# A recommendation tower on one core: ScalarE takes over the normalization of 12 of 26 features

## The chip, the core and the metric

The kernel runs on one core of a Trainium2 chip. The core has five engines that run side by side and meet through semaphores: TensorE (PE; its weight loads are PEld), VectorE (DVE), ScalarE (ACT), GpSimd (POOL) and SyncE (SP). The metric is the device time of one launch in microseconds (us), lower is better. Three runs of the kernel before took 626.68, 628.12 and 629.10 us.

## What is computed

The batch has 2048 samples, each with a dense vector of 256 numbers and 26 table lookups of 64 numbers (all float32). Cut to what matters:

```python
e = stack([tbl_f[ids[:, f]] for f in range(26)], axis=1)          # 2048 x 26 x 64
x = layer_norm(dense @ Wd.T, gd, bd)                              # 2048 x 128
y = layer_norm(einsum('bnd,ed->bne', e, Ws), gs, bs)              # each feature projected and normalized
y = layer_norm(einsum('bne,pn->bep', y, Wsi), gsi, bsi)           # 26 features mixed into 32
T = concat([x, y])                                                # 33 vectors of 128
Z = T @ T^T, its lower triangle (528)                             # pairwise products
out = layer_norm(Zflat @ Wl.T, gl, bl), the first 384 of 512
h = relu([out, dense] @ W_top1 + b_top1); h = relu(h @ W_top2 + b_top2); y = h @ W_top3
```

The first layer norm of a feature needs a factor per sample and feature, one over a standard deviation. The kernel finds that deviation without projecting: it takes a quadratic form of the gathered row, and then scales the gathered row itself. That scaling, row times factor, is what the change moves.

## The kernel before

**Tiles and quarters.** The 2048 samples are 16 tiles `t` of 128 (one sample per partition). Every engine runs the same outer loop, `for h in range(QUARTERS)`, over quarters `h`, 83 in all. A tile enters at `h = 4t` and passes through stages at fixed distances (the constants `MEASURE = 1` to `STORE = 22`), so that some six tiles are in work at once. `tile(h, at)` gives the tile whose once-per-tile stage `at` falls into this quarter, `part(h, at)` the tile and the quarter (0 to 3) of a stage that comes four times per tile. There is no scheduler: each engine executes its steps in the order in which they are written in its loop, and waits where a semaphore has not come far enough. In this text "quarter 0 to 3" is `h` modulo 4; a tile's norms fall into `h = 4t+1` to `4t+4`.

**Gathers (L255).** GpSimd issues 26 indirect DMAs per tile, one per feature, into `emb[t % 2]`, in four batches of 8, 6, 6 and 6. A batch waits for `gram_done` (the pairwise products of some eight quarters back) and for `nrm_ready` (that the buffer's last user, two tiles back, has been read).

**Norms.** TensorE transposes the gathered batch into `b_a` (L312), ScalarE copies it to `embt` (L494), TensorE multiplies with a Gram matrix into `b_a` (L321), VectorE multiplies with `emb` (`prod`, L757) and sums (`var_n`, L761); every second quarter it clips the result (`var_m`, L767) and ScalarE takes the root (`std_n`, L500).

**Normalization.** VectorE's `normalize(t, k)` takes the reciprocals (`rstd_n`, L774) and scales two features per instruction into `nrm` (L778): seven instructions for features 0 to 13 (k = 0) in quarter 3, six for features 14 to 25 (k = 1) in the quarter 1 two quarters later. `nrm` is laid out as 64 x 32, features innermost, so each feature is written at steps of 32 numbers (128 bytes). Then `shuffle(t)` transposes `nrm` into `byn` (L788), which the mixing of the following four quarters reads.

**Mixing and projection, four times per tile.** TensorE mixes into `b_mix` (L330), ScalarE copies to `mixed` (L505), TensorE projects into `b_y` (L342), VectorE adds the bias (`yb`, L793), ScalarE squares (`sq`, L510), VectorE sums (`var_y`, L800), ScalarE takes the root (`std_y`, L515, a quarter later), VectorE takes the reciprocal (L805) and scales into `V` (L811, four instructions), TensorE forms the products `b_z` (L354), ScalarE copies to `zs` (L521).

**Once per tile.** The dense vector's branch ends in ScalarE's `xn` (L541, quarter 3), TensorE's transpose of it (L377), and ScalarE's `V` (L551) and `xt` (L554) at the head of quarter 0. In quarter 0 VectorE also rearranges `zs` (L822 to L825). TensorE interacts in quarter 1 (L396, ten matmuls), and runs the top network's layers (L418, L425, L434) for an older tile over all four quarters; this begins at `h = 18`. ScalarE's `zt` (L559, L561) and `h` (L586, L592) belong to them. In the first eleven quarters VectorE also prepares weights.

TensorE's order inside a quarter is: transpose of `xn`, transposes of the batch, mixing, norms, projection, layers, products. `b_a` and `b_mix` are single buffers, so ScalarE's copies stand between TensorE's steps.

Of the kernel before, what the change touches and what calls it, by code (L numbers as in the profile page):

```python
# [35 lines left out]
HALVES = [range(0, 14), range(14, 26)]  # L36

# [4 lines left out]
DENSE_NORM = 3  # L42
# [28 lines left out]
def tower(nc, a, out):  # L71
# [4 lines left out]
    with ExitStack() as ctx:  # L76
# [6 lines left out]
        def sem(name):  # L83
# [68 lines left out]
        prod_done, varn_done, varm_done, stdn_done, rstdn_done, nrm_ready, byn_ready = (  # L152
            sem("prod_done"), sem("varn_done"), sem("varm_done"), sem("stdn_done"), sem("rstdn_done"), sem("nrm_ready"), sem("byn_ready"))
# [88 lines left out]
        def _(pool):  # L242
# [4 lines left out]
            for t in range(T):  # L247
                if t < 2:
                    pool.wait_ge(idx_loaded[t], 16)
                for b in range(4):  # L250
                    after(pool, nrm_ready, 2 * (t - 2) + b // 2 + 1)

                    after(pool, gram_done, 4 * t + b - PROJECT - 2)
                    for f in features(b):
                        pool.indirect_dma_start(out=emb[t % 2][:, f, :], out_offset=None, in_=tables[f],  # L255
                                                in_offset=bass.IndirectOffsetOnAxis(ap=idx[:, t, f:f + 1], axis=0)
                                                ).then_inc(gathered[t % 2][b], 16)
# [220 lines left out]
        def _(act):  # L478
# [22 lines left out]

            def copy_mixed(t, c):
                act.wait_ge(mix_done, 4 * t + c + 1)
                after(act, proj_done, 4 * t + c - 1)
                nc.scalar.activation(mixed[c % 2][:, :], b_mix[:, :], ACT.Copy).then_inc(mixed_copied, 1)  # L505
# [92 lines left out]
            for h in range(QUARTERS):  # L598
# [13 lines left out]
                if (last := part(h, PROJECT + 2)):  # L612
                    copy_zs(*last)
                if (t := tile(h, DENSE)) is not None:
                    copy_dt(t)
                if bc:
                    square_y(*bc)
                if ab and ab[1] % 2:
# [15 lines left out]
                if (t := tile(h, DENSE_NORM)) is not None:  # L634
                    scale_x(t)
                if h == 1:
# [3 lines left out]
        def _(dve):  # L640
# [128 lines left out]
            def normalize(t, k):  # L769
# [3 lines left out]
                after(dve, nrm_ready, 2 * (t - 1) + k + 1)  # L773
                nc.vector.reciprocal(rstd_n[:, f0:f0 + n], std_n[:, f0:f0 + n]).then_inc(rstdn_done, 1)  # L774
                dve.wait_ge(rstdn_done, 2 * t + k + 1)
                after(dve, byn_ready, 2 * t)
                for f in range(f0, f0 + n, 2):
# [4 lines left out]
            def shuffle(t):  # L782

                dve.wait_ge(nrm_ready, 2 * (t + 1))
                after(dve, mix_done, 4 * (t - 1))
# [108 lines left out]
```

## Time and profile before

| | |
|---|---|
| median of 3 runs | 628.12 us |
| the profiled execution | 628.74 us |
| its span | 626.9 us |
| TensorE busy | 520.4 us (83%) |
| VectorE busy | 519.8 us (83%) |
| GpSimd busy | 402.9 us (64%) |
| ScalarE busy | 295.3 us (47%) |
| the 208 scalings into `nrm` | 51.9 us, 384 ns each |

The profile is of one execution. "Busy" is the time in which an engine had an instruction of its own in work; neighbouring instructions of one engine overlap a little, so durations summed are more than the time they take up. The pause behind a wait is put down to what released it.

### The profile page before, as it was taken

The numbers are of one execution on the slowest core, as the hardware profiler recorded it, in microseconds if no ns is written. First come the engines' busy times: TensorE is split into PE (matmuls) and PEld (weight loads), VectorE is DVE, ScalarE is ACT, GpSimd is POOL, SyncE is SP. The second block draws the span as 40 slices with busy tenths as digits, with TensorE's granted clock in tenths as the row PEclk, the third lists the DMA queues.
The fourth block names the chain that finished last, engine by engine and source line by source line (L and its number), as shares of the span: only waits on it lengthen the run. The fifth ranks groups of instructions, "written<-read, shape, count | busy, mean of one in ns | idle before, by whom it ended". The sixth has DMA issues, their size and how long they took to land.

```text
span 626.9 us, 17592 instructions
## 1 busy us (share of the span) xinstructions
PE 520.4 (83%) x6955; PEld 394.3 (63%) x6955; DVE 519.8 (83%) x1073; ACT 295.3 (47%) x730; POOL 402.9 (64%) x422
## 2 busy tenths in 40 slices
PE   1462777777899999999998899899998989979886
PEld 1352556545576767676767677676776676747665
DVE  3499689899999999999998979999999898986500
ACT  0410343445465556464636445555555464635422
POOL 6777775767777777777777777777777777200000
PEclk9955887798999999999999899999999999999999
DMA  7311111111111111111111111111111111000000
GB/s 176 109 24 33 27 28 30 28 34 27 35 28 36 28 37 27 37 28 31 34 28 36 29 36 27 37 27 37 28 36 28 29 27 28 14 1 2 2 1 1
DMA packets 22610, 20.22 MB, mean 32 GB/s; under 512 B 12017, under 2 KB 14721, under 8 KB 22529
## 3 DMA queue, kind: packets, MB, share of 16 engines
q0 software_dynamic: 13312, 13.66, 12.1%
q1 hardware_dynamic: 8400, 4.33, 2.7%
q8 instruction: 55, 0.90, 0.6%
q10 hardware_dynamic: 816, 1.11, 0.6%
q14 instruction: 27, 0.21, 0.1%
HBM read 19.07 MB, written 0.01 MB: 30 GB/s over the span
## 4 chain that ended last, share of the span: by engine, by line
PE 37%; DVE 24%; issue 16%; ACT 8%; POOL 8%; DMA 3%; SPq 2%; ACTq 0%; DVEq 0%; POOLq 0%
PE b_l L418 10%; POOL emb L255 8%; PE b_y L342 7%; PE b_l L396 5%; DVE nrm L778 3%; DVE byn L788 3%; DVE V L811 3%; DVE yb L793 3%; DVE var_y L800 3%; PE b_a L321 3%; PE b_z L354 3%; DVE prod L757 2%; DMA emb<-in_tbl,idx 2%; ACT mixed L505 2%; PE b_a L312 2%
## 5 line engine op out<-in xcount | busy, mean ns | idle before, releaser
L255 POOL DMA_INDIRECT emb<-in_tbl,idx x416 | 402.2, 967 | 134.7 <-issue 118.5
L510 ACT ACTIVATE sq<-yb 128x1024 f32<-128x1024 f32 x64 | 67.7, 1059 | 191.1 <-DVE yb L793 187.2
L342 PE MATMUL b_y<-mixed,projw 64*128 64x512 f32 x256 | 74.9, 663 | 23.8 <-ACT mixed L505 23.8
L793 DVE TENSOR_TENSOR yb<-b_y,bias_y 128x1024 f32<-128x1024 f32 x64 | 78.1, 1220 | 19.9 <-PE b_y L342 19.5
L811 DVE TENSOR_TENSOR V<-yb,rstd_y 128x256 f32<-128x256 f32 x256 | 91.9, 422 | 2.2
L800 DVE TENSOR_REDUCE var_y<-sq 128x32 f32<-128x1024 f32 x64 | 77.8, 1215 | 6.9 <-ACT sq L510 5.6
L396 PE MATMUL b_l<-wlt,zt 128*128 128x512 f32 x160 | 72.9, 603 | 0.5 <-ACT zt L561 0.5
L330 PE MATMUL b_mix<-mix,byn 128*128 128x128 f32 x512 | 72.4, 287 | 0.0
L321 PE MATMUL b_a<-gram_w,embt 128*128 128x128 f32 x416 | 66.3, 303 | 6.3 <-ACT embt L494 5.6
L354 PE MATMUL b_z<-V 128*32 128x34 f32 x4096 | 58.2, 200 | 12.5 <-DVE V L811 9.7
L330 PEld LDWEIGHTS b_mix<-mix,byn 128*128 128x128 f32 x512 | 66.4, 203 | 0.2
L354 PEld LDWEIGHTS b_z<-V 128*32 128x32 f32 x4096 | 49.1, 110 | 24.9 <-DVE V L811 9.3
L321 PEld LDWEIGHTS b_a<-gram_w,embt 128*128 128x128 f32 x416 | 57.5, 211 | 11.5 <-ACT embt L494 10.2
L788 DVE STREAM_TRANSPOSE byn<-nrm 128x1024 f32<-128x1024 f32 x32 | 59.3, 1927 | 0.5
L312 PE MATMUL b_a<-ident,emb 128*128 128x128 f32 x208 | 38.5, 303 | 22.4 <-DVE prod L757 16.1
L494 ACT ACTIVATE embt<-b_a 128x512 f32<-128x512 f32 (+1 forms) x64 | 33.0, 516 | 49.6 <-PE b_a L312 49.3
L396 PEld LDWEIGHTS b_l<-wlt,zt 128*128 128x128 f32 x160 | 29.1, 190 | 42.9 <-issue 42.1
L418 PE MATMUL b_l<-z_t,w 128*128 128x128 f32 x384 | 54.1, 278 | 0.0
L778 DVE TENSOR_TENSOR nrm<-emb,rstd_n 128x128 f32<-128x128 f32 x208 | 51.9, 384 | 1.1
L418 PEld LDWEIGHTS b_l<-z_t,w 128*128 128x128 f32 x384 | 48.9, 195 | 0.0
L418 PE MATMUL b_l<-dt,w 128*128 128x128 f32 x256 | 41.6, 286 | 0.9 <-ACT y_sb L596 0.9
L312 PEld LDWEIGHTS b_a<-ident,emb 128*128 128x128 f32 x208 | 25.6, 153 | 26.0 <-issue 18.1
(131 smaller groups left out, 681.7 us busy)
## 6 DMA issues: line engine op xcount, KB each, us to landing
emb<-in_tbl,idx POOLq DMA_INDIRECT x416
dense<-in_r_dense_t SPq DMA_DIRECT2D x16, 128.0 KB, 2.3
V<-in_L_rec_Wl ACTq DMA_DIRECT2D x1, 1056.0 KB, 5.2
w<-in_W_top SPq DMA_DIRECT2D x2, 512.0 KB, 7.0
w<-in_W_top SPq DMA_DIRECT2D x1, 768.0 KB, 5.3
out_y<-y_sb SPq DMA_DIRECT2D x16, 0.5 KB
idx<-in_ids SPq DMA_DIRECT2D x1, 195.0 KB, 5.1
wd<-in_L_rec_Wd SPq DMA_DIRECT2D x1, 128.0 KB, 4.1
```

Source lines behind the costliest of these rows:

```text
L255: pool.indirect_dma_start(out=emb[t % 2][:, f, :], out_offset=None, in_=tables[f], in_offset=bass.IndirectOffsetOnAxis(ap=idx[:, t, f:f + ...
L312: last = nc.tensor.transpose(b_a[:, n * P:(n + 1) * P], emb[t % 2][:, 2 * c:2 * c + 2, :].rearrange("p n d -> p (n d)"), ident[:, :])
L321: last = nc.tensor.matmul(b_a[:, n * P:(n + 1) * P], embt[:, n, :], gram_w[:, :], start=True, stop=True)
L330: last = nc.tensor.matmul(b_mix[:, m * P:(m + 1) * P], byn[t % 2][:, j:j + 2, :].rearrange("p j d -> p (j d)"), mix[:, :], start=True, sto ...
L342: last = nc.tensor.matmul(b_y[:, j2, :], projw[r, :], mixed[c % 2][r, :], start=True, stop=True, tile_position=(64 * j2, 0))
L354: last = nc.tensor.matmul(b_z[32 * q:32 * q + 32, GRAM * j:GRAM * (j + 1)], v[:, 0:NP], v, start=True, stop=True)
L396: last = nc.tensor.matmul(b_l1[:, :], zt[:, c, :], wlt[:, c, :], start=(c == 0), stop=(c == RC - 1))
L418: last = nc.tensor.matmul(dst, w1[:, c, m * P:(m + 1) * P], rhs, start=(n == 0), stop=(n == 4))
L788: nc.vector.transpose(byn[t % 2][:, :, d].rearrange("p j d -> p d j"), nrm[:, d, :]).then_inc(byn_ready, 1)
L793: nc.vector.tensor_tensor(yb[c % 2][:, :, :, :].rearrange("e h s p -> e (h s) p"), b_y[:, :, :].rearrange("e h (s p) -> e (h s) p", p=NP), ...
L800: nc.vector.tensor_reduce(var_y[c % 2][:, :], sq[:, :, :, :].rearrange("e h s p -> e (h s) p"), AXX, ALU.add).then_inc(vary_done, 1)
L811: last = nc.vector.tensor_tensor(V[t % 2][:, j2, c, m:m + 2, :, 0:NP].rearrange("e m q p -> e (m q) p"), yb[c % 2][:, j2, 4 * m:4 * m + 8, :],
```

## The change

In the order of the program: two constants, a semaphore `act_nrm`, a wait on it for GpSimd's first batch of a tile, ScalarE's own `normalize(t, lo, hi)`, its four calls, and on VectorE the shorter loop with two waits on `act_nrm`. ScalarE's version handles one feature per instruction (128 x 64, with the factor as a per-partition scale), where VectorE's handles two. VectorE keeps features 12 and 13 in the first half and all of the second.

```diff
--- before.py
+++ after.py
@@ -34,6 +34,9 @@
 
 BATCHES = [range(0, 4), range(4, 7), range(7, 10), range(10, 13)]
 HALVES = [range(0, 14), range(14, 26)]
+
+ACT_FEATURES = 12
+ACT_PIECES = 4
 
 
 
@@ -149,8 +152,8 @@
 
         gathered = [[sem(f"gathered{h}{b}") for b in range(4)] for h in range(2)]
         emb_transposed, embt_copied, gw_done = sem("emb_transposed"), sem("embt_copied"), sem("gw_done")
-        prod_done, varn_done, varm_done, stdn_done, rstdn_done, nrm_ready, byn_ready = (
-            sem("prod_done"), sem("varn_done"), sem("varm_done"), sem("stdn_done"), sem("rstdn_done"), sem("nrm_ready"), sem("byn_ready"))
+        prod_done, varn_done, varm_done, stdn_done, rstdn_done, nrm_ready, act_nrm, byn_ready = (
+            sem("prod_done"), sem("varn_done"), sem("varm_done"), sem("stdn_done"), sem("rstdn_done"), sem("nrm_ready"), sem("act_nrm"), sem("byn_ready"))
 
         mix_done, mixed_copied, proj_done = sem("mix_done"), sem("mixed_copied"), sem("proj_done")
         y_biased, y_squared, vary_done, stdy_done, rstdy_done, y_scaled = (
@@ -249,6 +252,8 @@
                     pool.wait_ge(idx_loaded[t], 16)
                 for b in range(4):
                     after(pool, nrm_ready, 2 * (t - 2) + b // 2 + 1)
+                    if b == 0:
+                        after(pool, act_nrm, ACT_PIECES * (t - 1))
 
                     after(pool, gram_done, 4 * t + b - PROJECT - 2)
                     for f in features(b):
@@ -499,6 +504,14 @@
                 after(act, rstdn_done, 2 * (t - 1) + k + 1)
                 nc.scalar.activation(std_n[:, f[0]:f[-1] + 1], var_m[:, f[0]:f[-1] + 1], ACT.Sqrt, bias=eps[:, 0:1]).then_inc(stdn_done, 1)
 
+            def normalize(t, lo, hi):
+
+                act.wait_ge(rstdn_done, 2 * t + 1)
+                after(act, byn_ready, 2 * t)
+                for f in range(lo, hi):
+                    last = nc.scalar.activation(nrm[:, :, f], emb[t % 2][:, f, :], ACT.Copy, scale=rstd_n[:, f:f + 1])
+                last.then_inc(act_nrm, 1)
+
             def copy_mixed(t, c):
                 act.wait_ge(mix_done, 4 * t + c + 1)
                 after(act, proj_done, 4 * t + c - 1)
@@ -611,10 +624,14 @@
                     copy_mixed(*bc)
                 if (last := part(h, PROJECT + 2)):
                     copy_zs(*last)
+                if (t := tile(h, DENSE_NORM + 1)) is not None:
+                    normalize(t, 4, 7)
                 if (t := tile(h, DENSE)) is not None:
                     copy_dt(t)
                 if bc:
                     square_y(*bc)
+                if (t := tile(h, DENSE_NORM + 1)) is not None:
+                    normalize(t, 7, 10)
                 if ab and ab[1] % 2:
                     deviation_n(ab[0], ab[1] // 2)
                 if (t := tile(h, LAYER2)) is not None:
@@ -633,6 +650,10 @@
                     relu1(t, 1)
                 if (t := tile(h, DENSE_NORM)) is not None:
                     scale_x(t)
+                if (t := tile(h, DENSE_NORM + 1)) is not None:
+                    normalize(t, 10, 12)
+                if (t := tile(h, DENSE_NORM)) is not None:
+                    normalize(t, 0, 4)
                 if h == 1:
                     prepare_wsq()
 
@@ -771,10 +792,12 @@
                 f0, n = HALVES[k][0], len(HALVES[k])
                 dve.wait_ge(stdn_done, 2 * t + k + 1)
                 after(dve, nrm_ready, 2 * (t - 1) + k + 1)
+                if k == 0:
+                    after(dve, act_nrm, ACT_PIECES * t)
                 nc.vector.reciprocal(rstd_n[:, f0:f0 + n], std_n[:, f0:f0 + n]).then_inc(rstdn_done, 1)
                 dve.wait_ge(rstdn_done, 2 * t + k + 1)
                 after(dve, byn_ready, 2 * t)
-                for f in range(f0, f0 + n, 2):
+                for f in range(max(f0, ACT_FEATURES), f0 + n, 2):
                     last = nc.vector.tensor_tensor(nrm[:, :, f:f + 2].rearrange("p d n -> p n d"), emb[t % 2][:, f:f + 2, :],
                                                    rstd_n[:, f:f + 2].unsqueeze(2).broadcast_to([P, 2, D]), ALU.mult)
                 last.then_inc(nrm_ready, 1)
@@ -782,6 +805,7 @@
             def shuffle(t):
 
                 dve.wait_ge(nrm_ready, 2 * (t + 1))
+                dve.wait_ge(act_nrm, ACT_PIECES * (t + 1))
                 after(dve, mix_done, 4 * (t - 1))
                 for k in range(2):
                     d = slice(k * D // 2, (k + 1) * D // 2)
```

**ScalarE, from quarter 3 into quarter 0 of a tile in mid-program.** `xn` closes quarter 3, `V` opens quarter 0. Before:

```order
L541 ACTIVATE xn<-b_x,r_x 128x128 [waits xt_done,x_rstd]
L551 ACTIVATE V<-b_x,bd,gd 128x4x16x2 [waits zt_done,gram_done,xt_done]
L554 ACTIVATE xt<-b_x,bd,gd 128x128
L494 ACTIVATE embt<-b_a 128x384 [waits gw_done,emb_transposed]
L515 ACTIVATE std_y<-var_y,eps 128x32 [waits rstdy_done,vary_done]
L505 ACTIVATE mixed<-b_mix 128x512 [waits proj_done,mix_done]
```

Now:

```order
L554 ACTIVATE xn<-b_x,r_x 128x128 [waits xt_done,x_rstd]
L512 ACTIVATE nrm<-emb,rstd_n 128x64 [waits byn_ready,rstdn_done]
L512 ACTIVATE nrm<-emb,rstd_n 128x64 x3
L564 ACTIVATE V<-b_x,bd,gd 128x4x16x2 [waits zt_done,gram_done,xt_done]
L567 ACTIVATE xt<-b_x,bd,gd 128x128
L499 ACTIVATE embt<-b_a 128x384 [waits gw_done,emb_transposed]
L528 ACTIVATE std_y<-var_y,eps 128x32 [waits rstdy_done,vary_done]
L518 ACTIVATE mixed<-b_mix 128x512 [waits proj_done,mix_done]
```

Four scalings stand between `xn` and `V`, and so ahead of `xt`, `embt`, `std_y` and `mixed` too.

**ScalarE, the rest of quarter 0 and the head of quarter 1.** The second `embt` (128x512) is the next quarter's. Before, from `sq` on:

```order
L510 ACTIVATE sq<-yb 128x1024 [waits vary_done,y_biased]
L500 ACTIVATE std_n<-var_m,eps 128x12 [waits rstdn_done,varm_done]
L592 ACTIVATE h<-b_l,b 128x128 [waits h2_done]
L592 ACTIVATE h<-b_l,b 128x128
L559 ACTIVATE zt<-b_l 128x512 [waits o_done,zt_done]
L561 ACTIVATE zt<-b_x 96x128 [waits zt_done]
L494 ACTIVATE embt<-b_a 128x512 [waits gw_done,emb_transposed]
L515 ACTIVATE std_y<-var_y,eps 128x32 [waits rstdy_done,vary_done]
```

Now, from `sq` on (a piece of three stands just ahead of it as well):

```order
L523 ACTIVATE sq<-yb 128x1024 [waits vary_done,y_biased]
L512 ACTIVATE nrm<-emb,rstd_n 128x64 [waits byn_ready,rstdn_done]
L512 ACTIVATE nrm<-emb,rstd_n 128x64 x2
L505 ACTIVATE std_n<-var_m,eps 128x12 [waits rstdn_done,varm_done]
L605 ACTIVATE h<-b_l,b 128x128 [waits h2_done]
L605 ACTIVATE h<-b_l,b 128x128
L572 ACTIVATE zt<-b_l 128x512 [waits o_done,zt_done]
L574 ACTIVATE zt<-b_x 96x128 [waits zt_done]
L512 ACTIVATE nrm<-emb,rstd_n 128x64 [waits byn_ready,rstdn_done]
L512 ACTIVATE nrm<-emb,rstd_n 128x64
L499 ACTIVATE embt<-b_a 128x512 [waits gw_done,emb_transposed]
L528 ACTIVATE std_y<-var_y,eps 128x32 [waits rstdy_done,vary_done]
```

Three more scalings stand between `sq` and `std_n`, and two between `zt` and the next quarter's `embt`. On VectorE the loop behind the reciprocals of quarter 3 has one instruction where it had seven; nothing else moves there.

## Rows read from the trace of the kernel before

**Rows 1.** The page, part 1: busy us (share of the span), instructions

```profile
PE 520.4 (83%) x6955; PEld 394.3 (63%) x6955; DVE 519.8 (83%) x1073; ACT 295.3 (47%) x730; POOL 402.9 (64%) x422
```

**Rows 2.** GpSimd's timeline: start us, us, instruction [idle before <-releaser]; last row its groups from 175.7 to 538.5

```profile
99.53 0.94 POOL L255 DMA_INDIRECT emb<-in_tbl,idx  x1 [3.63 <-PE b_z L354]
...
134.22 0.94 POOL L255 DMA_INDIRECT emb<-in_tbl,idx  x1 [2.13 <-PE b_z L354]
...
175.74 1.03 POOL L255 DMA_INDIRECT emb<-in_tbl,idx  x1 [1.50 <-PE b_z L354]
...
L255 POOL DMA_INDIRECT emb<-in_tbl,idx x286 | 275.8, 964 | 88.4 <-issue 80.5 <-PE b_z L354 7.6 <-DVE nrm L778 0.3
```

**Rows 3.** Waits from 176 to 540: us in total, times, longest us

```profile
PE b_a L312 <- DMA emb<-in_tbl,idx: 6.2, 6, 2.4
...
ACT std_y L515 <- DVE var_y L800: 2.2, 5, 0.6
```

**Rows 4.** Chain of work that ended last: start us, us, what

```profile
73.36 1.68 DVE nrm L778 x7
...
143.23 1.50 DVE nrm L778 x6
...
170.26 1.13 PE b_y L342 x4
...
202.29 1.13 PE b_y L342 x4
...
431.12 1.13 PE b_y L342 x4
...
463.39 1.13 PE b_y L342 x4
...
529.25 1.13 PE b_y L342 x4
```

**Rows 5.** Timeline of quarter 3 of a tile in mid-program: VectorE, then TensorE

```profile
371.77 1.75 DVE L778 TENSOR_TENSOR nrm<-emb,rstd_n 128x128 f32<-128x128 f32 x7
373.36 0.33 DVE L805 RECIPROCAL rstd_y<-std_y 128x32 f32<-128x32 f32 x1
...
375.14 1.21 DVE L793 TENSOR_TENSOR yb<-b_y,bias_y 128x1024 f32<-128x1024 f32 x1
...
373.94 1.13 PE L342 MATMUL b_y<-mixed,projw 64*128 64x512 f32 x4 [0.29 <-ACT mixed L505]
```

**Rows 6.** The same two engines in quarter 3 of tile 3

```profile
146.35 1.21 DVE L793 TENSOR_TENSOR yb<-b_y,bias_y 128x1024 f32<-128x1024 f32 x1
...
144.26 1.13 PE L342 MATMUL b_y<-mixed,projw 64*128 64x512 f32 x4 [0.42 <-ACT mixed L505]
```

**Rows 7.** ScalarE's timeline, from quarter 3 over quarters 0 and 1 into quarter 2

```profile
378.27 0.62 ACT L586 ACTIVATE h<-b_l,b1p 128x128 f32<-128x128 f32 x2
378.77 0.38 ACT L541 ACTIVATE xn<-b_x,r_x 128x128 f32<-128x128 f32 x1
379.56 0.59 ACT L551 ACTIVATE V<-b_x,bd,gd 128x128 f32<-128x128 f32 x1 [0.42 <-PE b_x L377]
...
384.11 1.07 ACT L510 ACTIVATE sq<-yb 128x1024 f32<-128x1024 f32 x1 [2.12 <-DVE yb L793]
385.42 0.30 ACT L500 ACTIVATE std_n<-var_m,eps 128x12 f32<-128x12 f32 x1 [0.25 <-DVE var_m L767]
...
386.85 0.60 ACT L494 ACTIVATE embt<-b_a 128x512 f32<-128x512 f32 x1
...
397.15 0.32 ACT L515 ACTIVATE std_y<-var_y,eps 128x32 f32<-128x32 f32 x1 [0.58 <-DVE var_y L800]
```

**Rows 8.** ScalarE's short instructions, start to start

```profile
22.38 4.83 ACT L487 ACTIVATE wsq<-V 128x4 f32<-128x4 f32 x40
...
380.64 0.32 ACT L515 ACTIVATE std_y<-var_y,eps 128x32 f32<-128x32 f32 x1
380.85 0.60 ACT L505 ACTIVATE mixed<-b_mix 128x512 f32<-128x512 f32 x1
```

## The prediction

> **What bounds the kernel now.** I read the page first. TensorE and VectorE are each busy 83% of the span, GpSimd 64%, ScalarE 47% [rows 1]. So it looks as if moving work from VectorE to ScalarE must pay. An average over stages doesn't say so; three more views do.
>
> GpSimd's timeline: three batches of gathers waited for the products `b_z` for more than the usual 0.30 us between two gathers (3.63, 2.13 and 1.50 us, that is 6.4 us above it); from 175.74 us to the last gather, which starts at 537.31 us, no other pause is over 0.31 us. Those 285 intervals take 361.6 us, 1.269 us each [rows 2]. A tile has 26 gathers: the stream can't go faster than 33.0 us per tile.
>
> The chain that ended last, read at `b_y` of each tile's quarter 2: where no gather was late, a tile takes between 202.29 - 170.26 = 32.03 us and 463.39 - 431.12 = 32.27 us; I take 32.15 [rows 4]. The eleven tiles from 170.26 to 529.25 take 358.99, where 11 x 32.15 = 353.65: 5.3 us went to late gathers, for which TensorE waited 6.2 us in six places [rows 3]. So from quarter 18 on two processes run at nearly one pace, the gather stream (33.0) and the loop through TensorE, ScalarE and VectorE (32.15), and the slower wins.
>
> Which VectorE work lies on the loop? The chain holds first-half scalings in the opening tiles (the seven at 73.36, six of the seven at 143.23) [rows 4], and none of quarter 3 later on. The timeline shows why. In quarter 3 of a late tile `yb` starts at 375.14, and `b_y`, which it needs, ends at 373.94 + 1.13 = 375.07 [rows 5]. If VectorE comes 1.4 us sooner, it waits for TensorE.
>
> **The change, part by part.**
>
> *1. Removed: six VectorE scalings per tile, in quarter 3.* Seven take from 371.77 to the next instruction at 373.36, so 0.227 us each and not their duration of 0.38; six are 1.36 us [rows 5]. Tiles 0 to 2 have VectorE as their limit (weights are prepared too): full gain, 3 x 1.36 = 4.1 us. In tile 3 `yb` starts at 146.35 and `b_y` ends at 144.26 + 1.13 = 145.39 [rows 6]: with 0.03 for the signal the gain is 0.93. From tile 4 on it is nothing, as above. Sum: **-5.0 us** at 170.26.
>
> *2. Added: twelve ScalarE scalings per tile, 128 x 64 with a per-partition factor.* No row has one. Start to start, `std_y` (32 columns, per-partition operand) is followed 0.21 us later [rows 8]; `h` (128 columns, the same) goes at 0.25, since two of them precede `xn` by 0.50 [rows 7]. At 64 columns that is about 0.225. They write at 128-byte steps, as the forty `wsq` copies do, which take 4.83 / 40 = 0.12 us each without a per-partition operand [rows 8]. I take **0.235 us**. Ends: 0.12 (the copies' pace) and 0.38 (`xn`'s whole duration [rows 7]); likelier ends are 0.21 and 0.28, since `std_y` lasts 0.32 and is followed after 0.21, so 0.11 of each duration overlaps and 0.38 becomes 0.27.
>
> The page "ScalarE: Activation LUTs", section "What ACT_TABLE_LOAD costs", of the Trainium skill gives 186 ns + 0.833 per column, 93 more for a per-partition operand, and 93 of overlap: 0.239 us as an estimate for this form. By it the sum below would be 0.4 us higher. The same skill's page "VectorE: DVE Perf Modes", section "The TRN2 errata", speaks against the change as such: each small instruction on SBUF pays a fixed latency again, so one should work on 512 elements or more. The copies' rows agree that the fixed part is most of it.
>
> *3. Where the twelve lie.* Walk one tile [rows 7], with 0.235 each.
> - Four between `xn` and `V`. ScalarE is free 0.28 after `xn`'s start, at 379.05; four end at 379.99; `V` started at 379.56. **+0.43 us.** Behind `V` in ScalarE's order stand `xt`, `embt`, `std_y` and `mixed`, on which TensorE's norms, its `b_y` and VectorE's next `V` wait, so all of quarter 0 is later by it.
> - Three ahead of `sq`: ScalarE waits 2.12 us there for `yb`, three take 0.7. Nothing. If `yb` came 1.4 us sooner they would still be hidden.
> - Three between `sq` and `std_n`: ScalarE is free 0.96 after `sq`'s start; 384.11 + 0.96 + 0.70 = 385.77, `std_n` started at 385.42. **+0.35 us.** VectorE doesn't feel it: it reads `std_n` only after `var_y`.
> - Two between `zt` and the next quarter's `embt`: **+0.47 us**. The last piece then ends some 0.4 us before VectorE reaches the shuffle, so its new wait costs nothing.
> - The 0.82 us of the last two delay quarter 1's `embt`, then TensorE's norms, `b_y`, ten interaction matmuls and products, without a gap, and so quarter 2's transposes and `embt`. There ScalarE had a margin: it waited for `var_y` before `std_y` (0.58 us here; 2.2 us in five tiles, 0.44 each [rows 3]). 0.82 - 0.44 = **+0.38 us**.
>
> Together the loop grows by 0.43 + 0.38 = 0.81 us, to 32.96. Eleven times: **+8.9 us**. The 1.36 us that VectorE has saved turn into waits for `b_y` in quarter 3.
>
> *4. Late gathers.* The stream's pauses of 6.4 us shrink, since its gates come up to 5.0 us sooner; it runs some 4.3 us ahead of today and can't go faster. The loop, at 32.96 per tile from 165.3, reaches the last tile's gathers about 1.4 us ahead of today, so the gathers are there: the **-5.3 us** are saved.
>
> *5. The end.* The last tile's quarter 3 to 0 crossing comes after those eleven: **+0.4 us**. Quarter 65 has no batch to transpose, so the other delay has nothing behind it.
>
> *GpSimd's new wait* (`act_nrm`, first batch of a tile) is met when the piece in quarter 4(t-1) is done, some three quarters before that batch's gate on `b_z`: nothing. VectorE's wait in front of the reciprocals is met one tile earlier: nothing.
>
> **Sum: -5.0 + 8.9 - 5.3 + 0.4 = -1.0 us**, against the profiled execution's 628.74 (span 626.9 and 1.8 around it). The median of the runs is 0.6 lower, 628.12; so I forecast **627.1 us**. A difference of 0.5% (3.1 us) is about what a measurement can tell from none. The sum moves by 1.0 us for each 0.01 us of the ScalarE scaling (nine of them on the loop, eleven tiles): 0.21 gives 624.6, 0.28 gives 631.7.
>
> **The rivals.**
> - *Pieces hidden, gathers bound.* If a scaling takes 0.20 us or the margins are wider, the loop is faster than the stream, and the gathers set the end: 4.3 us sooner, plus the end's 0.4, so about 624. For it: the two paces are 0.04 us apart in my own sum. Against: `xn` to `V` has no room. It is also the floor, as the stream has only 6.4 us of pauses to lose.
> - *VectorE is the bound after all.* All 16 tiles gain 1.36 us: -22, 606 us. Against: rows 5, and a gather stream that can't follow.
> - *ScalarE becomes the bound.* Slower by over 0.5% once a scaling takes more than 0.275 us: strided writes with a per-partition factor are in no row, and each piece opens with waits. The place is `xn` to `V` and `std_n` to `embt`. At 0.30 us: 9 x 0.065 x 11 = 6.4 us above my sum, 633.5. For it: everything ScalarE does there is waited for by TensorE, at once. If the VectorE page's rule were the whole story, more and smaller instructions for fewer and larger, this is what one would see.
> - *The change doesn't do what it says:* the first half's VectorE instructions would have to stay. The order shows one left of seven, so I give this nothing.
>
> **How the numbers follow.** Forecast, within 0.5%: 0.48. Gather-bound and faster: 0.25; VectorE-bound: 0.03. ScalarE-bound and slower: 0.24. The range takes the likelier ends of the scaling (624.6 and 631.7), the floor of the gather-bound case with 1.5 us for an error in the opening, 622.5, and the 0.30 case, 634.0.
>
> **What the profile after would show.** Right: `nrm` on ScalarE every 0.22 to 0.25 us; `b_y` of tile 4's quarter 2 near 165.3 (now 170.26); 32.8 to 33.1 us per tile afterwards; VectorE's busy share down with new waits for `b_y` in quarter 3; no or few waits for gathers; ScalarE no longer waiting for `var_y` in quarter 2. Wrong: a loop that stays at 32.15, or a last gather before 532 us, or waits of the shuffle or of GpSimd for ScalarE.

## The result, and the profile after

The changed kernel takes 622.48 us (median of 5 runs, 621.45 to 623.0). The kernel before, run beside it, takes 626.68 us (5 runs, 625.34 to 629.1). The ratio is 0.9924, with a 95% interval of 0.9901 to 0.9946: **faster by 0.8%**. The forecast, 627.1 us and no change that can be measured, was wrong, and the median lies 0.02 us below its range. What happened is close to the first rival, "Pieces hidden, gathers bound", at about 624.

The profiled execution took 623.0 us with a span of 621.2. Part 1 of its page, beside [rows 1], and the chain that ended last by engine and its largest line:

```profile
span 621.2 us, 17751 instructions
...
PE 515.5 (83%) x6955; PEld 390.6 (63%) x6955; DVE 501.3 (81%) x977; ACT 334.1 (54%) x922; POOL 403.1 (65%) x422
...
PE 27%; POOL 25%; issue 18%; DVE 17%; ACT 7%; DMA 3%; SPq 2%; ACTq 0%; DVEq 0%; POOLq 0%
POOL emb L260 25%; PE b_l L423 7%; PE b_y L347 5%; PE b_l L401 4%; DVE yb L817 2%; DVE byn L812 2%; PE b_z L359 2%; PE b_a L326 2%; DVE V L835 2%; SPq L211 2%; PE b_l L430 2%; DVE var_y L824 2%; ACT mixed L518 2%; PE b_a L317 2%; PE b_mix L335 1%
```

VectorE is busy 18.5 us less and ScalarE 38.8 us more, so the work has moved as the diff says. The span fell by 5.7 us. The chain now stands on the gathers for a quarter of the span; before, their share was 8% (`POOL emb L255 8%`).

GpSimd's timeline, to set against [rows 2]: after the first gather one pause is left that is clearly above the usual 0.30 or 0.31 us, in the opening; then the last gather.

```profile
96.72 0.94 POOL L260 DMA_INDIRECT emb<-in_tbl,idx  x1 [0.52 <-issue]
...
531.21 0.94 POOL L260 DMA_INDIRECT emb<-in_tbl,idx  x1 [0.30 <-issue]
```

The pauses of 3.63, 2.13 and 1.50 us are gone, and the last gather starts at 531.21 instead of 537.31 us: 6.1 us sooner, where the three pauses were 6.4 us too long in all. From that start to the end of the span it is 90.0 us, and was 89.6. So the whole gain of the profiled execution lies ahead of the last gather. How much of it is the change, and how much differs between any two executions, is taken up under e4_clock_kept.

TensorE's timeline, `b_y` of quarter 2 of tiles 4, 5 and 15, and the first transposes of tile 15's gathered rows:

```profile
162.67 1.13 PE L347 MATMUL b_y<-mixed,projw 64*128 64x512 f32 x4 [1.35 <-ACT mixed L518]
...
195.24 1.13 PE L347 MATMUL b_y<-mixed,projw 64*128 64x512 f32 x4 [0.63 <-ACT mixed L518]
...
510.94 0.66 PE L317 MATMUL b_a<-ident,emb 128*128 128x128 f32 x4 [0.74 <-DMA emb<-in_tbl,idx]
...
523.20 1.13 PE L347 MATMUL b_y<-mixed,projw 64*128 64x512 f32 x4 [0.61 <-ACT mixed L518]
```

Against [rows 4] tile 4 comes 7.6 us sooner (162.67 for 170.26), tile 15 only 6.05 (523.20 for 529.25). A tile without a wait for a gather takes 195.24 - 162.67 = 32.57 us; over all eleven the mean is (523.20 - 162.67) / 11 = 32.78.

The waits from 176 to 540 us, beside [rows 3]:

```profile
DVE rstd_y L829 <- ACT std_y L528: 24.2, 34, 0.9
...
DVE yb L817 <- PE b_y L347: 11.4, 22, 0.7
...
PE b_a L326 <- ACT embt L499: 6.4, 14, 0.5
PE b_a L317 <- DMA emb<-in_tbl,idx: 6.0, 9, 0.9
```

TensorE still waits 6.0 us for gathers, now in nine short places instead of six that go up to 2.4 us. The wait of `std_y` for `var_y` is gone; VectorE's reciprocals, which waited 13.4 us for ScalarE before, now wait 24.2.

ScalarE's timeline in mid-program, beside [rows 7], in quarter 3 and the quarter after it:

```profile
370.73 0.38 ACT L554 ACTIVATE xn<-b_x,r_x 128x128 f32<-128x128 f32 x1
370.98 1.13 ACT L512 ACTIVATE nrm<-emb,rstd_n 128x64 f32<-128x64 f32 x4
371.93 0.59 ACT L564 ACTIVATE V<-b_x,bd,gd 128x128 f32<-128x128 f32 x1
...
376.48 1.06 ACT L523 ACTIVATE sq<-yb 128x1024 f32<-128x1024 f32 x1 [1.49 <-DVE yb L817]
377.44 0.87 ACT L512 ACTIVATE nrm<-emb,rstd_n 128x64 f32<-128x64 f32 x3
378.16 0.29 ACT L505 ACTIVATE std_n<-var_m,eps 128x12 f32<-128x12 f32 x1
```

Four scalings take 371.93 - 370.98 = 0.95 us, 0.238 each; `V` follows `xn` after 1.20 us instead of 0.79, and `std_n` follows `sq` after 1.68 instead of 1.31.

### The profile page after: what moved, and what is told of

Same layout as the page of the kernel before. It is cut to its first block, busy times and chain, and to the rows that moved or that the text cites. A ratio compares the mean times of both kernels' runs of the same rounds, so it can differ in the third digit from the quotient of the medians.

```text
span 621.2 us, 17751 instructions
## 1 busy us (share of the span) xinstructions
PE 515.5 (83%) x6955; PEld 390.6 (63%) x6955; DVE 501.3 (81%) x977; ACT 334.1 (54%) x922; POOL 403.1 (65%) x422
## 4 chain that ended last, share of the span: by engine, by line
PE 27%; POOL 25%; issue 18%; DVE 17%; ACT 7%; DMA 3%; SPq 2%; ACTq 0%; DVEq 0%; POOLq 0%
POOL emb L260 25%; PE b_l L423 7%; PE b_y L347 5%; PE b_l L401 4%; DVE yb L817 2%; DVE byn L812 2%; PE b_z L359 2%; PE b_a L326 2%; DVE V L835 2%; SPq L211 2%; PE b_l L430 2%; DVE var_y L824 2%; ACT mixed L518 2%; PE b_a L317 2%; PE b_mix L335 1%
## 5 line engine op out<-in xcount | busy, mean ns | idle before, releaser
L347 PE MATMUL b_y<-mixed,projw 64*128 64x512 f32 x256 | 73.6, 652 | 20.4 <-ACT mixed L518 20.4
L335 PE MATMUL b_mix<-mix,byn 128*128 128x128 f32 x512 | 70.6, 283 | 0.0
L326 PEld LDWEIGHTS b_a<-gram_w,embt 128*128 128x128 f32 x416 | 56.1, 207 | 21.3 <-ACT embt L499 20.1
L335 PEld LDWEIGHTS b_mix<-mix,byn 128*128 128x128 f32 x512 | 64.7, 198 | 0.2
L512 ACT ACTIVATE nrm<-emb,rstd_n 128x64 f32<-128x64 f32 x192 | 56.2, 411 | 0.0
L829 DVE RECIPROCAL rstd_y<-std_y 128x32 f32<-128x32 f32 x64 | 21.5, 337 | 30.0 <-ACT std_y L528 29.9
```

What stands on the lines that cost most here:

```text
L326: last = nc.tensor.matmul(b_a[:, n * P:(n + 1) * P], embt[:, n, :], gram_w[:, :], start=True, stop=True)
L335: last = nc.tensor.matmul(b_mix[:, m * P:(m + 1) * P], byn[t % 2][:, j:j + 2, :].rearrange("p j d -> p (j d)"), mix[:, :], start=True, sto ...
L347: last = nc.tensor.matmul(b_y[:, j2, :], projw[r, :], mixed[c % 2][r, :], start=True, stop=True, tile_position=(64 * j2, 0))
```

## The experiments

The forecast sum had three parts that could be wrong: the opening, the loop, and the gathers. **Theory A** (the gather stream sets the end): whatever relieves VectorE in the first tiles lets the stream run without its pauses, and nothing else counts. **Theory B** (steady relief): VectorE's relief pays in all tiles. **Theory C** (clock): part of the gain is TensorE's clock in the opening. Each ratio below is to the kernel before, run on the same chip (medians of 626.56 us beside e1 to e4, 626.84 beside e5 to e8, 626.58 beside e9 to e12), with its 95% interval.

### e1_relief_alone: VectorE relieved, ScalarE given nothing

```diff
 # the kernel before, VectorE's scalings; nrm is set to zero once at the start
-                for f in range(f0, f0 + n, 2):
+                for f in range(max(f0, 12), f0 + n, 2):
```

> The kernel before, with the first 12 features' scalings left out altogether (nrm is zero there), so VectorE is relieved and ScalarE gets nothing. Stream theory (the gathers run without a pause and set the end; what counts is only how early the opening stage lets them go): quarter 18's b_y about 7.5 us earlier than before, loop at 32.15 us or at the stream's 32.9 per tile, last gather near 531, end 5.5 to 6.5 us faster than before, within 1 us of the changed kernel. Steady-relief theory (VectorE's saved 1.4 us per tile is a gain in every tile, and ScalarE's pieces give some back): 12 to 20 us faster.

Measured: 621.4 us (620.76 to 622.77), ratio 0.9921 [0.9888, 0.9955]. GpSimd pauses nowhere, and the end looks like that of the changed kernel:

```profile
162.02 0.70 PE L342 MATMUL b_y<-mixed,projw 64*128 64x512 f32 x2 [1.41 <-ACT mixed L505]
...
521.95 1.13 PE L342 MATMUL b_y<-mixed,projw 64*128 64x512 f32 x4 [0.61 <-ACT mixed L505]
```

The relief alone gives 5.2 us. ScalarE's whole added work costs about 1 us on top of it by the medians (621.4 and 622.48), which the intervals of the two ratios don't settle. Theory B, by which 22 us were to be had, falls.

### e2_late_only and e3_early_only: the change in tiles 4 to 15, and in tiles 0 to 3

```diff
 # the changed kernel, in ScalarE's normalize; the waits on act_nrm count to match
+                if t not in ACT_TILES:
+                    return
 # in VectorE's normalize
-                for f in range(max(f0, ACT_FEATURES), f0 + n, 2):
+                for f in range(max(f0, ACT_FEATURES if t in ACT_TILES else 0), f0 + n, 2):
```

> ScalarE's normalization for tiles 4 to 15 only; tiles 0 to 3 as before. Stream theory: the opening is as before (quarter 18's b_y near 170.3, GpSimd's three pauses of 6.4 us stay), and from there on the loop takes 32.6 per tile for 32.15, which stands against gathers at 33.0 that cost 5 us already: end within 1.5 us of before. Steady-relief theory: 12 tiles relieved, 3 us or more faster than before.

> ScalarE's normalization for tiles 0 to 3 only; tiles 4 to 15 as before. Stream theory: quarter 18's b_y near 162.7, last gather near 531, end as the changed kernel or up to 0.5 us faster (no four scalings in the last crossing from quarter 3 to 0). Steady-relief theory: slower than the changed kernel, since 12 of 16 tiles lose the relief, 3 us or more.

Measured: late only 626.94 us (623.84 to 627.53, 10 runs), ratio 0.9991 [0.9967, 1.0015]; early only 623.58 (622.3 to 625.95, 10 runs), ratio 0.9945 [0.9926, 0.9965]. Of the two parts the early one carries the gain, as theory A has it. In twelve tiles of sixteen the change does nothing that can be measured.

But the two ends are not reached in the same way. In e3_early_only TensorE waits 14.5 us for gathers from 176 us on. In e2_late_only its transposes wait once:

```profile
PE b_a L322 <- DMA emb<-in_tbl,idx: 1.2, 1, 1.2
```

Gathers have 4% of its chain. Its loop enters at 167.96 us, takes (527.36 - 167.96) / 11 = 32.67 us per tile and is itself the limit: what it no longer waits for gathers, ScalarE's pieces take.

Early alone is 1 us behind the full change, within the spread of both.

The last gathers of the two, late first:

```profile
534.81 1.14 POOL L265 DMA_INDIRECT emb<-in_tbl,idx  x1 [0.30 <-issue]
```

```profile
532.16 1.06 POOL L265 DMA_INDIRECT emb<-in_tbl,idx  x1 [0.30 <-issue]
```

To the ends of their spans (625.3 and 622.7) it is 90.5 us in both. As e2_late_only hardly waits for gathers, such a constant distance doesn't tell by itself which of the two processes set the end.

### e4_clock_kept: the kernel before, with matmuls put into TensorE's idle time of the opening

```diff
 # the kernel before, TensorE
+                after(pe, zs_copied, 4 * t + c)
+                if (t, c) in ((1, 0), (2, 0)):
+                    for _ in range(6):
+                        nc.tensor.matmul(b_z[:, 384:512], ident[:, :], ident[:, :], start=True, stop=True)
                 pe.wait_ge(y_scaled, 4 * t + c + 1)
-                after(pe, zs_copied, 4 * t + c)
 ...
+                if h in (12, 16):
+                    pe.wait_ge(prod_done, h - 1)
+                    for _ in range(3):
+                        nc.tensor.matmul(b_a[:, 0:P], ident[:, :], ident[:, :], start=True, stop=True)
```

> The kernel before, with nothing moved to ScalarE, and idle time of TensorE filled by matmuls on unused or free PSUM columns (six ahead of the products of quarters 11 and 15, three at the head of quarters 12 and 16). Clock theory (2.6 of the 7.6 us that the opening gained is TensorE at 2.4 instead of 1.2 GHz in quarters 12 and 16): granted clock near 1.0 in 116 to 122 (0.51 before), quarter 18's b_y 2 to 3 us earlier than 170.26, one of GpSimd's pauses shorter, end 1.5 to 2.5 us faster. If the clock has no part: 0 us.

Measured: 626.49 us (624.82 to 629.34, 10 runs), ratio 1.0008 [0.9985, 1.003]. This was a miss: no gain in the median. In the profiled execution the edit did what it was to do: from 116 to 122 us the granted clock is 1.00 where it was 0.51, `b_y` of tile 4's quarter 2 starts at 166.23 us (170.26 before), GpSimd's first two pauses are 1.59 and 0.81 us (3.63 and 2.13), and the span is 3.2 us shorter. The ten runs don't bear that gain out.

So the execution of before that was profiled is itself a poor base. What the granted clock did in the opening, by stretches (us, busy of each engine, PEclk, DMA share, GB/s), in the profiled executions of before, of the changed kernel, of e2_late_only (whose work up to tile 4's quarter 2 is that of before), and of this one:

```profile
36.00:56.00 20.00, 8.92 (x37) 7.36 (x36) 19.33 (x41) 2.46 (x6) 15.43 (x16) 0.50 0.13 24
56.00:84.00 28.00, 17.71 (x148) 14.15 (x150) 21.75 (x48) 8.30 (x19) 21.29 (x23) 0.68 0.16 32
```

```profile
36.00:56.00 20.00, 9.05 (x37) 7.49 (x37) 19.33 (x40) 5.13 (x18) 15.46 (x15) 1.00 0.15 25
56.00:84.00 28.00, 19.61 (x218) 15.15 (x218) 20.85 (x39) 10.23 (x27) 21.26 (x23) 0.88 0.17 31
```

```profile
36.00:56.00 20.00, 8.83 (x36) 7.28 (x36) 19.33 (x41) 2.46 (x6) 15.43 (x16) 1.00 0.12 24
```

```profile
36.00:56.00 20.00, 9.13 (x38) 7.58 (x37) 19.37 (x40) 2.46 (x6) 15.59 (x15) 1.00 0.13 25
56.00:84.00 28.00, 17.14 (x196) 13.43 (x197) 22.57 (x51) 8.30 (x19) 21.13 (x23) 0.94 0.16 32
```

TensorE is granted 0.50 of full speed (1.2 GHz) between 36 and 56 us in the profiled execution of before, and full speed (2.4 GHz) in the other three. Its own work there is the same (the matmuls that were put in come later) and so is its busy time, 8.9 of 20 us in before and 8.8 to 9.1 in the others. So the half clock is not bound to the kernel, and differs between executions.

What it costs is another question. In e2_late_only `b_y` of tile 4's quarter 2 starts at 167.96 us, 2.3 us sooner than in before's trace, with the same work up to there. But the pair e7_batches and e8_batches_early (below), which also do the same work up to there, has it the other way round:

```profile
36.00:56.00 20.00, 8.80 (x36) 7.25 (x36) 19.32 (x40) 5.04 (x18) 15.66 (x15) 1.00 0.15 31
```

```profile
36.00:56.00 20.00, 5.76 (x22) 4.25 (x21) 19.29 (x40) 5.03 (x18) 15.43 (x16) 0.50 0.15 30
```

e7, the first, has full speed and reaches `b_y` of tile 4's quarter 2 at 165.07 us; e8 has the half clock and reaches it at 162.22. So executions with one and the same opening differ by 1.2 to 2.9 us at tile 4 (the changed kernel run again, e12, is at 161.50 where the first profile has 162.67), and the half clock from 36 to 56 us isn't shown to be the reason.

The mean clock of a whole run doesn't rank the runs either. Of the 50 runs of before beside the experiments, six with 0.946 took 628.6 to 629.0 us and nine with 0.983 or 0.984 took 624.5 to 625.5. But 23 with 0.975 took 625.4 to 629.0 (median 626.6), and two with 0.958 took 624.1 and 624.9. Nine of the ten runs with the added matmuls had 0.981 to 0.989 and gained nothing. The profiled execution on which the forecast stands, 628.74 us at 0.946, is one of the slow ones. So the base of the forecast was 2 us too slow. For theory C nothing is left that the medians show: the interval of this run allows matmuls that keep the clock a gain of 0.9 us at most (0.9985).

### e5_b24 and e6_a24: fewer gathers, before and changed

```diff
 # both: GpSimd gathers features 24 and 25 for tiles 0 and 1 alone; TensorE's wait for the last batch counts to match
+                        if t > 1 and f > 23:
+                            continue
```

> The kernel before, with features 24 and 25 gathered only for tiles 0 and 1 (later tiles reuse old rows there): 24 gathers per tile, so the stream takes 30.5 us per tile and can't bind. Stream theory: the loop's own pace shows, 32.0 to 32.3 us per tile from quarter 18 on, no waits for gathers, end 4 to 6 us faster than before.

> The changed kernel, with the same gathers left out. Stream theory: the loop's own pace with ScalarE's twelve pieces, 32.5 to 32.7 us per tile (0.4 above e5_b24), end 1.5 to 2.5 us faster than the changed kernel, 8 us faster than before. Walk as predicted (0.81 per tile): 32.95 per tile, end as the changed kernel. Steady-relief theory: a pace below 32.15.

Measured: 618.62 us for before (617.39 to 621.97), ratio 0.9877 [0.9808, 0.9947]; 616.69 for the changed kernel (615.63 to 617.49), ratio 0.9833 [0.977, 0.9896]. Both gain more than was expected: e5 8.2 us where 4 to 6 were, e6 5.8 us of the changed kernel's time where 1.5 to 2.5 were. From 176 us on no transpose waits for a gather in either, so here is the loop by itself, as the forecast's step 3 wants it. `b_y` of tiles 4 and 15, before and then changed:

```profile
165.84 0.70 PE L344 MATMUL b_y<-mixed,projw 64*128 64x512 f32 x2 [1.41 <-ACT mixed L507]
...
518.00 0.70 PE L344 MATMUL b_y<-mixed,projw 64*128 64x512 f32 x2 [1.34 <-ACT mixed L507]
```

```profile
160.21 0.70 PE L349 MATMUL b_y<-mixed,projw 64*128 64x512 f32 x2 [1.34 <-ACT mixed L520]
...
517.52 0.70 PE L349 MATMUL b_y<-mixed,projw 64*128 64x512 f32 x2 [0.61 <-ACT mixed L520]
```

The loop takes 352.16 / 11 = 32.01 us before and 357.31 / 11 = 32.48 changed: **+0.47 us per tile**, not +0.81. And the opening gains 5.6 us. Set beside the two profiles of the changed kernel, e6's eleven tiles are 3.2 and 4.6 us shorter (357.31, where the first has 360.53 and e12 has 361.95): that much of the changed kernel's loop is the gathers'. ScalarE's timeline from quarter 3 to the next quarter 2 tells where the 0.34 us between the two figures went; before:

```profile
369.96 0.38 ACT L543 ACTIVATE xn<-b_x,r_x 128x128 f32<-128x128 f32 x1
370.76 0.59 ACT L553 ACTIVATE V<-b_x,bd,gd 128x128 f32<-128x128 f32 x1 [0.42 <-PE b_x L379]
...
378.04 0.60 ACT L496 ACTIVATE embt<-b_a 128x512 f32<-128x512 f32 x1
...
387.52 0.49 ACT L496 ACTIVATE embt<-b_a 128x384 f32<-128x384 f32 x1 [0.44 <-PE b_a L314]
388.31 0.32 ACT L517 ACTIVATE std_y<-var_y,eps 128x32 f32<-128x32 f32 x1 [0.31 <-DVE var_y L802]
```

and changed:

```profile
366.97 0.38 ACT L556 ACTIVATE xn<-b_x,r_x 128x128 f32<-128x128 f32 x1
...
376.21 0.59 ACT L501 ACTIVATE embt<-b_a 128x512 f32<-128x512 f32 x1
...
385.44 0.49 ACT L501 ACTIVATE embt<-b_a 128x384 f32<-128x384 f32 x1 [0.84 <-PE b_a L319]
385.83 0.32 ACT L530 ACTIVATE std_y<-var_y,eps 128x32 f32<-128x32 f32 x1
```

TensorE's `b_y` and products of quarter 1 lie between the two `embt`, and so does the start of VectorE's `var_y`, for which `std_y` waits; before, then changed:

```profile
379.78 1.13 PE L344 MATMUL b_y<-mixed,projw 64*128 64x512 f32 x4
385.77 1.01 PE L356 MATMUL b_z<-V 128*32 128x34 f32 x64
387.07 1.21 DVE L802 TENSOR_REDUCE var_y<-sq 128x32 f32<-128x1024 f32 x1
```

```profile
377.94 1.13 PE L349 MATMUL b_y<-mixed,projw 64*128 64x512 f32 x4
383.94 0.77 PE L361 MATMUL b_z<-V 128*32 128x34 f32 x64
384.59 1.21 DVE L826 TENSOR_REDUCE var_y<-sq 128x32 f32<-128x1024 f32 x1
```

Count from `xn` (the medians of nine tiles are the same to 0.01 us). Quarter 1's `embt` comes after 8.08 us before and 9.24 changed, +1.16; `V` has 0.41 of it. TensorE carries this on: `b_y` is +1.15 and the products start at +1.16. But the 64 products take 0.77 us now and took 1.01, so their end is +0.92, and quarter 2's `embt` +0.91 (17.56 and 18.47). Why they took longer before, no wait in the profile says. `std_y` behind it is only +0.51 (18.35 and 18.86): it had waited for `var_y`. It follows `var_y` by 0.03 us still (384.59 + 1.21 = 385.80), and `var_y` itself is +0.51. So two paths meet in `std_y` of the changed kernel, ScalarE's with its margin used up and VectorE's, and the profile's chain takes VectorE's in this tile, in e5 as in e6. Of the 0.51, 0.41 is the four scalings ahead of `V`.

### e7_batches and e8_batches_early: the 8 gathers of the first batch made 6

```diff
 # the changed kernel; e8 has e3's ACT_TILES = range(0, 4) as well
-BATCHES = [range(0, 4), range(4, 7), range(7, 10), range(10, 13)]
+BATCHES = [range(0, 3), range(3, 7), range(7, 10), range(10, 13)]
```

> The changed kernel with the large gather batch second instead of first (3, 4, 3, 3 pairs for 4, 3, 3, 3). Stream theory: quarter 1's transposes wait for two gathers fewer, so the tightest batch has 1.6 us more room; the stream itself stays at 33.0 per tile: 1 to 1.6 us faster than the changed kernel. If the gathers' order had no part in the end: within 0.3 us.

> The batches of e7_batches together with ScalarE's normalization in tiles 0 to 3 only. Stream theory: the loop is back at 32.15 and has more room behind the stream: 1.6 to 2.5 us faster than the changed kernel. Else as e7_batches.

Measured: 621.28 us (619.62 to 623.11, 4 runs), ratio 0.9899 [0.9831, 0.9967]; and 622.7 (619.9 to 624.1, 10 runs), ratio 0.992 [0.9891, 0.995]. Neither can be told from the changed kernel, though e7's median is 1.2 us lower. In e7's profile no transpose waits for a gather from 176 us on, and the loop runs at its own 32.60 us per tile; but it enters at 165.07 and so ends where the changed kernel does, at 523.72. Both were inconclusive: the second batch has eight gathers now, GpSimd pauses for 1.51 us at 97.8 us, where the changed kernel pauses for 0.52, and what the loop gains may be lost there. That isn't shown: e8 has the same batches, has no such pause and enters at 162.22.

### e9_no_scalings: VectorE relieved twice over

```diff
 # the kernel before, VectorE's scalings; nrm is set to zero once at the start
-                for f in range(f0, f0 + n, 2):
+                for f in range(f0 + n - 2, f0 + n, 2):
```

> The kernel before with 24 of its 26 scalings left out (only the last of each half is kept, and nrm is zero elsewhere): the first features of both halves are not normalized. VectorE's work falls by about 5 us more per tile than in the run that left out the first 12. If the gather stream sets the end once VectorE is relieved a little, nothing more is gained than by leaving out 12: median 620 to 622 us, last gather issued at 530 to 531, no pause of GpSimd after tile 0. If VectorE's load still set the pace of the loop or of the opening, the time would fall well below, to 612 or less.

Measured: 618.89 us (617.69 to 619.76, 4 runs), ratio 0.9867 [0.9839, 0.9895]. That is 2.5 us below e1, where theory A had allowed next to nothing, and far from the 612 that VectorE's pace would give. The last gather of its profile:

```profile
529.46 0.94 POOL L255 DMA_INDIRECT emb<-in_tbl,idx  x1 [0.30 <-issue]
```

It is 0.5 us sooner than e1's (529.96), so up to there the second relief has bought next to nothing, as theory A has it. The rest of the span, 88.5 us, is 1.1 shorter than e1's 89.6. Behind the last gather the stream binds no longer, and VectorE's relief may count there; but the changed kernel run again (e12, below) has 88.4 us without it, so that isn't shown, and 0.9 us between the medians has no place in the traces at all.

### e10_hidden, e11_hidden_batches and e12_changed_again: the four scalings moved from `V`'s way

```diff
 # the changed kernel, ScalarE's order in quarter 3
+                if (t := tile(h, DENSE_NORM)) is not None:
+                    normalize(t, 0, 4)
 ...
-                if (t := tile(h, DENSE_NORM)) is not None:
-                    normalize(t, 0, 4)
```

The upper place is ahead of the copies and the square, where ScalarE waits for `yb` anyway; the lower one is between `xn` and `V`. e11 adds e7's batches; e12 is the changed kernel once more.

> The changed kernel with its piece of four scalings (features 0 to 3 of the next tile) moved from between xn and V to ahead of the copy and the square of that quarter. The step-3 reading (four scalings between xn and V delay the quarter by 0.41 us): V follows xn at 0.80 us again, a tile without a gather wait takes 32.1 to 32.2. Since the gather stream ends the program, it gains 0 to 0.8 us of the changed kernel's time, near 622.0. If the scalings delay the quarter wherever they stand, V still follows late or rstd_y does, and the time is that of the changed kernel or up to 2 us more.

> The same with the gathers of tile 0's preparation issued in batches of 3, 4, 3, 3 pairs as in e7_batches, where the loop waited for no gather and ran at 32.60 us per tile. If the gathers and the 0.41 us between xn and V are two limits close together, taking both away gives more than either: 1.5 to 2 us under the changed kernel, near 620.5. If the gathers alone count, it is that of e7_batches, 621.3; if it is below neither, both readings lack a third limit near 32.6 us per tile.

> The changed kernel once more, on the same chip as the two runs beside it, as their base: 621.5 to 623.0 us.

Measured, 6 runs each on one chip: 621.66 us for e10 (621.4 to 622.44, ratio 0.9922 [0.9901, 0.9944]), 621.09 for e11 (619.14 to 621.52, ratio 0.9904 [0.988, 0.9927]), 622.62 for e12 (621.46 to 623.97, ratio 0.9937 [0.9913, 0.9961]). In e10's timeline `V` follows `xn` after 0.80 us, and a tile without a late gather takes 259.45 - 227.30 = 32.15 (others 32.15 to 32.41):

```profile
372.03 0.38 ACT L554 ACTIVATE xn<-b_x,r_x 128x128 f32<-128x128 f32 x1
372.83 0.58 ACT L564 ACTIVATE V<-b_x,bd,gd 128x128 f32<-128x128 f32 x1 [0.42 <-PE b_x L382]
```

```profile
227.30 0.70 PE L347 MATMUL b_y<-mixed,projw 64*128 64x512 f32 x2 [0.61 <-ACT mixed L518]
...
259.45 1.13 PE L347 MATMUL b_y<-mixed,projw 64*128 64x512 f32 x4 [0.61 <-ACT mixed L518]
```

So the loop is nearly back at its old pace with all twelve scalings on ScalarE. The program gains 1.0 us of the changed kernel (e12, on the same chip), just over the 0.8 expected, though eleven tiles at 0.42 us would be 4.6: the stream takes the rest. In e11 both limits show in one trace: the tiles from 164.42 to 389.93 us take 32.2 each, the last four from there to 521.63 take 32.9. It is 1.5 us under the changed kernel and the lowest median of the kernels that compute everything; against e12 the ranges overlap by 0.06 us, against e10 the difference of 0.6 us isn't settled.

## Why the prediction was wrong

Point by point, against the forecast's own steps.

1. **Step 1, -5.0 us in the opening: about right, on another base.** The trace has -7.6 us (170.26 to 162.67). 2.3 us of it lie between two executions of before's work: e2_late_only is at 167.96, and 167.96 - 162.67 = 5.3. The pair e5 and e6 has 5.6. As e12 is at 161.50, the figure isn't known to better than 1 us. The forecast compared the profiled execution with the median of three runs and took the difference of 0.6 for all there was; over 26 runs the median is 626.56, 2.2 us lower.
2. **Step 2, 0.235 us: right.** Measured 0.238. The Trainium skill's page "ScalarE: Activation LUTs", section "What ACT_TABLE_LOAD costs", gives 0.239 for this form by the estimate in the prediction; the trace agrees within 2 ns. By the rule of the Trainium skill's page "VectorE: DVE Perf Modes", section "The TRN2 errata", each small instruction on SBUF pays a fixed latency again, so the change was to hurt. The trace agrees on the busy time (38.8 us of ScalarE's for 192 instructions in place of 18.5 of VectorE's for 96) and not on the kernel's: the loop pays 0.47 us per tile for it, and the opening gains more.
3. **Step 3, the walk, failed at one term.** `xn` to `V` +0.43 (measured 0.41), `sq` to `std_n` +0.35 (0.37) and three ahead of `sq` for nothing were right. The failure is the last item: the 0.82 was to run "without a gap" through quarter 1, with one margin of 0.44 in quarter 2, so +0.38. In e5 and e6 the delay arrives as 0.75 at quarter 1's `embt`, and TensorE hands on that much up to the products. There 0.24 is lost, so that quarter 2's `embt` is 0.50 later, and the margin at `std_y` is 0.40: 0.10 is left. VectorE's `var_y`, whose path the walk did not price, is later by the same 0.10. With the 0.41 of `V` that is 0.51; the loop's mean grows by 0.47, and not 0.81. What shortens the products stays open.
4. **Step 3's sum, 32.96, was to be just under the stream's 33.0; the loop takes 32.57.** (The 33.0 is the pace of before's gathers; in e1 they go at 32.84, so it wasn't the stream's floor.) So the sum came from one pace that does not bind and "the 5.3 us are saved", while in fact 6.0 us of waits for gathers stay. Both errors have opposite signs: from tile 4 to tile 15 the forecast has +8.9 - 5.3 = +3.6, the trace 360.53 - 358.99 = +1.5.
5. **Step 5, +0.4: not settled.** From `b_y` at tile 15 to the end of the span it is 97.65 us before and 98.0 after. But the changed kernel run again (e12) has 96.45: two executions of one kernel differ there by four times the term.

The sum against the profiled execution was -5.0 + 3.6 + 0.4 = -1.0; the trace has -7.6 + 1.5 + 0.4 = -5.7. Of the 4.7 us between them 2.1 are the loop (steps 3 and 4), 0.3 the opening, and 2.3 the base: an execution of before 2.2 us above the median of its kernel. The other miss is a matter of weighing: the rival "gathers bound" was given 0.25 although the sum itself put it 0.04 us per tile away. Its price, 4.3 us sooner less 0.4 at the end, is near the difference of the medians, 4.2; with a base that differs by 2 us between executions, so near a hit is in part luck. Its floor of "6.4 us of pauses to lose" fits the trace, whose last gather starts 6.1 us sooner.

The signs named beforehand speak the same way: "a last gather before 532 us" was to show the forecast wrong, and it starts at 531.21. Of the signs for the forecast, `nrm` every 0.238 us and the `std_y` wait that is gone came true; `b_y` of tile 4 near 165.3 and "no or few waits for gathers" did not. One small slip in the sum: 0.28 us per scaling gives 631.6, not 631.7.

What isn't settled: how much of the 4.2 us between the medians is clock. Before at 0.983 takes 624.5 to 625.5 us, which would leave 2 to 3 us for the work, yet e4_clock_kept has those clocks at 626.49, so the mean clock alone doesn't rank the runs. That the opening carries the gain is shown by e2 and e3. Why e9, with its second relief, is 2.5 us below e1 stays open. That the gathers hold back the changed kernel's loop is shown by e6, whose eleven tiles without them are 3.2 to 4.6 us shorter, and by e10, whose loop by itself is 0.4 us per tile faster and whose time is 1.0 us shorter. The margin is thin, though: in e2 and e7 the loop's own pace, 32.6 to 32.7 us, is enough to keep it behind the stream, and TensorE waits for gathers 1.2 us and not at all. Both end 90.5 and 87.8 us behind their last gather like the others. Whether a stream with larger gathers would also move the 88 to 90 us behind it wasn't tried.

## What to carry to other kernels

Where two processes run at nearly one pace, cost a change by the slower one's milestones (here the last gather and what follows it), and only then by the loop: a relief that lets the stream start without pauses is worth about the pauses. When a delay is walked through a chain, walk every engine's path to the point where they meet, not only the path of the engine that gets the work: here VectorE's `var_y` set `std_y` before and after. And check the walk by counting from one instruction in both traces, since a delay can shrink where the list of waits names nothing, as the 0.24 us at the products. Compare the profiled execution with many runs before it serves as the base of a sum, and profile the same kernel twice before a difference of 1 or 2 us in one stage is given a reason.

## What was not expected of the hardware

- TensorE was granted half its clock from 36 to 56 us in the profiled execution of before and all of it in e2_late_only, with the same work up to there; tile 4 came 2.3 us later in before. e8_batches_early had the half clock and e7_batches all of it, again with the same work, and there tile 4 came 2.9 us sooner with the half clock.
- The time from the start of the last gather to the end of the span is 87.8 to 90.5 us in every kernel here that issues all gathers (89.6 before), with a mean of 32.5 us per tile in the loop ahead of it (e11) as with 33.0 (e3). In the changed kernel's two profiles it is 90.0 and 88.4: `b_y` of tile 15 to the end takes 98.0 us in the one, with a granted clock of 0.66 from 555 to 560 us, and 96.45 in the other, with 1.00.
- From tile 4 on a tile's first transposes start 1.5 to 2.4 us after the issue of the eighth gather ends in the changed kernel's trace. But one batch near 345 us was late in several other traces. TensorE waited for it 2.40 us in before, 2.58 in e1, 2.20 in e10, 2.28 in e12, only 0.60 in the changed kernel's profile, and not at all in e2 and e7:

```profile
353.06 0.66 PE L312 MATMUL b_a<-ident,emb 128*128 128x128 f32 x4 [2.40 <-DMA emb<-in_tbl,idx]
```

```profile
347.81 0.66 PE L317 MATMUL b_a<-ident,emb 128*128 128x128 f32 x4 [2.28 <-DMA emb<-in_tbl,idx]
```

- ScalarE's scalings, which write at 128-byte steps, last 0.39 to 0.45 us each but follow one another after 0.238: the duration alone would have priced them 1.7 times too high.
